# Mean and variance of four chunks through a quadratic form, and their z normalised straight out of PSUM, in a two-layer convolution kernel

## The chip, the cores and the metric

The kernel runs on one NeuronCore of a Trainium2 chip. A NeuronCore has a matrix engine (TensorE, PE in the profile), three engines for elementwise work (VectorE = DVE, ScalarE = ACT, GpSimd = POOL), SyncE (SP), which here only issues DMAs, and 16 DMA engines that all issuing engines share. Every engine works through its own instructions in order and waits on semaphores for the others. The metric is the device time of one execution in microseconds (us), and its median over several executions.

## The reference, cut to what matters

Two images of 1024 channels and 64 x 64 pixels pass two layers. Layer 0 is a deformable convolution block: a 1x1 convolution to 256 channels, a 3x3 convolution for the offsets, a bilinear gather at nine displaced places per pixel, a 1x1 convolution back to 1024 channels, with residual and ReLU. Layer 1 is what the change touches most:

```python
t = einsum('oc,bchw->bohw', Wt, x)   # 512 channels; p and g likewise
y = _rbf_kernel(t, p, g)             # a polynomial of second degree in t, with three sums per image as coefficients
z = einsum('oc,bchw->bohw', Wz, y)   # 512 -> 1024 channels
mu = mean(z, axis=(1, 2, 3)); var = mean((z - mu) ** 2, axis=(1, 2, 3))
zn = (z - mu) * rsqrt(var + EPS) * gn_w + gn_b
return zn + x
```

Mean and variance go over a whole image, so no z of an image can be normalised before all of its z is known, or at least its sum and its sum of squares.

## The kernel before, in words

Products are taken in a rounded format (fp32r). For precision every operand is split into a high part (ScalarE copies it to fp32r) and a low part (VectorE subtracts the high part), and a product is three matmuls: high x high, high weight x low, low weight x high (`product`, L194 to L196). The 8192 pixels of both images are 16 chunks of 512 (8 per image); a chunk of z has 8 tiles of 128 channels x 512 pixels, so there are 128 tiles, numbered through, and image 1 starts at tile 64. One tile is 4 x 3 = 12 matmuls of 512 columns.

The order of the work is written out by hand, as loops in one function for each engine:

- **Front (0 to about 665 us).** For each chunk: first convolution, nine products with w2 whose results (V) ScalarE copies out of PSUM and SyncE stores to memory (`store_v`), and the offsets (`offsets`, `select`, `y_shift`, `offs`). After each four chunks VectorE computes a table of gather places and weights, in three parts: `table_places`, `table_weights`, `table_entries`. GpSimd gathers with indirect DMAs (L631, L635), and VectorE and ScalarE weight and add what was gathered (`f_gather`).
- **Middle (about 665 to 1895 us).** For each chunk c the twelve groups of products g, p, t (`project`, q = 0 to 11), the rest of the gathers (`p_gather`), and layer 0's last convolution for the next chunk: `transposes` at q = 0 and 3, `o2` on ScalarE, `o2_low` on VectorE, `expand_pair` from q = 5. In chunk 0 the weights of the twelve groups are still being loaded in pieces `stage(w)`, w = 2 to 13, into three buffers in turn, by ScalarE's queue; ScalarE and VectorE split each piece (`split_high`, `split_low`). Pieces 5 and 6 are split ahead of q = 0.
- **End (about 1895 us on).** For each chunk GpSimd loads t into one buffer (TB). y is formed in four slices k: ScalarE scales (`y_scale`, L892), VectorE multiplies (`y_square`, L1319), ScalarE takes the high part (`y_high`, L904), VectorE the low one (`y_low`, L1323). TensorE forms z; ScalarE copies each tile to SBUF (`z_evict`, L967), VectorE takes its statistics (`stats`, L1367). z stays in SBUF, in a ring of 71 tiles. While z of image 1 is formed, image 0 is finished: a tile of x1 is loaded, VectorE forms z*a + x1 (`add_x1`, L1402), ScalarE adds the bias (`fin`, L975), SyncE stores (L548). How many tiles have been added by each z tile is written down in `adds_by`. After the last z tile come the statistics of image 1 (`fin_mean`, `fin_scale`), and then all 64 tiles of image 1 are added and stored.

```python
            for i in range(IMGS * ZT):            # ScalarE
                if zc + 1 < ALLC and k == KIN - 2:
                    for kk in range(KCP):
                        y_high(zc + 1, kk)
                z_evict(i)
```

## Time and profile before

| what | value |
|---|---|
| median of 3 runs | 2354.85 us (2352.66 to 2355.01) |
| the profiled execution's own time | 2349.92 us |
| its span, first to last instruction | 2348.1 us |
| TensorE busy | 2237.8 us, 95% of the span |
| VectorE, ScalarE, GpSimd busy | 67%, 53%, 33% |
| mean granted TensorE clock | 0.981 |
| DMA over the span | 284 GB/s |

The profile is that of one execution. Its span leaves out 1.8 us around it. TensorE's busy time counts overlapping matmuls once; in a stream each matmul is in the trace for 0.39 us, but the next one starts 0.23 us later, and it is this spacing that sums up to the time. A granted clock of 1.00 is 2.4 GHz, 0.50 is 1.2 GHz.

### The profile page before, as it was taken

Reading aid. Unit: us, or ns where it says so; the run is one execution under the profiler, and the core shown is the slowest. Engines: PE = TensorE matmul, PEld = TensorE weight load, DVE = VectorE, ACT = ScalarE, POOL = GpSimd, SP = SyncE. Lnnn points to the kernel's source line nnn. Section 1 sums busy time; section 2 is a strip of 40 time slices with the busy share of each in tenths; the row PEclk is TensorE's granted clock in tenths of the full one; section 3 lists DMA queues with packets and bytes.
Section 4 is the critical chain, followed back from the end, with each engine's and each line's share of the span. In section 5 each row is a group of like instructions: output and inputs, shape, how many; then the busy total and the mean of one; then the engine's idle time right before and its main releaser. Section 6 shows DMA issues by size and latency. Waiting matters only on the chain.

```text
span 2348.1 us, 29804 instructions
## 1 busy us (share of the span) xinstructions
PE 2237.8 (95%) x10252; PEld 1853.9 (79%) x10252; DVE 1573.3 (67%) x3177; ACT 1254.2 (53%) x2432; POOL 771.9 (33%) x706
## 2 busy tenths in 40 slices
PE   7999999999998999999999999999999999999970
PEld 6888888887877788888888888888888878887750
DVE  4213226667578988898889988898885324457855
ACT  6444444453455565656555655565553324446745
POOL 0100002333314555465567666766661000000000
PEclk9999999999999999999999999999999999999985
DMA  8988989999998998898889888988893111118869
GB/s 305 316 312 281 310 293 385 390 400 386 362 379 280 314 338 304 309 337 306 306 310 323 306 313 306 328 307 318 302 332 132 62 48 53 54 50 286 318 230 387
DMA packets 289823, 667.97 MB, mean 284 GB/s; under 512 B 27112, under 2 KB 101608, under 8 KB 283528
## 3 DMA queue, kind: packets, MB, share of 16 engines
q0 software_dynamic: 88048, 322.81, 39.0%
q1 hardware_dynamic: 171240, 257.87, 31.0%
q10 hardware_dynamic: 30384, 85.39, 9.8%
q8 instruction: 81, 1.33, 0.2%
q14 instruction: 70, 0.57, 0.1%
HBM read 435.47 MB, written 230.49 MB: 284 GB/s over the span
## 4 chain that ended last, share of the span: by engine, by line
PE 83%; DVE 7%; DMA 6%; SPq 1%; ACT 1%; issue 1%; POOL 0%; ACTq 0%; DVEq 0%
PE bank L194 22%; PE bank L196 22%; PE bank L195 22%; PE bank L1458 5%; PE bank L1459 5%; PE bank L1460 5%; DVE z L1402 2%; DMA xs<-x 2%; PE bank L1476 2%; DVE a L1029 1%; DMA g<-vwide,tbl 1%; DMA stage<-in_wl 1%; DMA xin<-in_x 1%; DVE zst L1367 1%; PE bank L1500 0%
## 5 line engine op out<-in xcount | busy, mean ns | idle before, releaser
L631 POOL DMA_INDIRECT g<-vwide,tbl x512 | 583.4, 1139 | 542.5 <-DVE a L1029 234.1
L194 PE MATMUL bank<-x1h,wlh 128*128 128x512 f32 x1536 | 603.1, 393 | 2.5 <-DVE x1l L1291 2.5
L196 PE MATMUL bank<-x1h,wll 128*128 128x512 f32 x1536 | 600.2, 391 | 0.0
L195 PE MATMUL bank<-x1l,wlh 128*128 128x512 f32 x1536 | 599.5, 390 | 0.0
L1029 DVE SCALAR_TENSOR_TENSOR a<-g,tbl,a 128x256 f32<-128x256 f32 x1224 | 527.6, 477 | 23.1 <-DMA g<-vwide,tbl 19.4
L658 ACT ACTIVATE g<-g,tbl 128x256 f32<-128x256 f32 x1008 | 426.9, 499 | 212.7 <-DMA g<-vwide,tbl 173.9
L194 PEld LDWEIGHTS bank<-x1h,wlh 128*128 128x128 f32 x1536 | 288.7, 188 | 62.9 <-issue 2.7
L196 PEld LDWEIGHTS bank<-x1h,wll 128*128 128x128 f32 x1536 | 288.7, 188 | 62.3
L195 PEld LDWEIGHTS bank<-x1l,wlh 128*128 128x128 f32 x1536 | 289.0, 188 | 60.8
L737 ACT ACTIVATE vb<-bank 128x512 f32<-128x512 f32 (+1 forms) x320 | 174.5, 554 | 193.4 <-PE bank L1460 168.9
L1458 PE MATMUL bank<-w2h,o1h 128*128 128x512 f32 (+1 forms) x640 | 237.3, 371 | 0.0
L1459 PE MATMUL bank<-w2l,o1h 128*128 128x512 f32 (+1 forms) x640 | 236.5, 369 | 0.0
L1460 PE MATMUL bank<-w2h,o1l 128*128 128x512 f32 (+1 forms) x640 | 236.0, 369 | 0.0
L1084 DVE TENSOR_TENSOR xl<-xin,xh 128x1024 fp32r<-128x1024 f32 x64 | 78.3, 1225 | 214.1 <-ACT xh L709 213.9
L194 PE MATMUL bank<-yh,wzh 128*128 128x512 f32 x512 | 203.3, 397 | 4.0 <-DVE yl L1323 2.8
L196 PE MATMUL bank<-yh,wzl 128*128 128x512 f32 x512 | 202.0, 395 | 0.0
L195 PE MATMUL bank<-yl,wzh 128*128 128x512 f32 x512 | 201.6, 394 | 0.0
L635 POOL DMA_INDIRECT g<-vone,tbl x128 | 152.8, 1194 | 132.0 <-DVE a L1013 101.0
L1367 DVE BATCH_NORM_STATS2 zst<-z 128x6 f32<-128x512 f32 x128 | 87.3, 689 | 103.5 <-ACT z L967 103.4
L646 POOL DMA_DIRECT2D tb<-t x16 | 8.7, 544 | 447.4 <-DVE yl L1323 436.2
L1291 DVE TENSOR_TENSOR x1l<-xf,x1h 128x512 fp32r<-128x512 f32 x128 | 83.9, 687 | 104.1 <-ACT x1h L858 104.1
L1010 DVE TENSOR_TENSOR a<-a,g 128x512 f32<-128x512 f32 x224 | 152.7, 682 | 0.0
(154 smaller groups left out, 3273.6 us busy)
## 6 DMA issues: line engine op xcount, KB each, us to landing
vwide<-vb SPq DMA_DIRECT2D x256, 256.0 KB, 4.7
vwide<-vb SPq DMA_DIRECT2D x112, 512.0 KB, 4.4
xf<-in_x SPq DMA_DIRECT2D x32, 1024.0 KB, 5.5
x<-xf ACTq DMA_DIRECT2D x32, 1024.0 KB, 7.1
out<-z SPq DMA_DIRECT2D x128, 256.0 KB, 5.3
xin<-in_x ACTq DMA_DIRECT2D x54, 512.0 KB, 5.6
t<-ts ACTq DMA_DIRECT2D x64, 256.0 KB, 4.9
tb<-t POOLq DMA_DIRECT2D x16, 1024.0 KB, 5.2
```

The lines of the kernel that those rows point to most:

```text
L194: nc.tensor.matmul(out, wh, xh, start=first, stop=False)
L195: nc.tensor.matmul(out, wh, xl, start=False, stop=False)
L196: return nc.tensor.matmul(out, wl, xh, start=False, stop=last)
L631: pool.indirect_dma_start(slot[:].rearrange("p a c -> p (a c)"), None, d["vwide"][img], bass.IndirectOffsetOnAxis(ap=at[:, i, tap(u), 0:1] ...
L635: pool.indirect_dma_start(slot[:, 2 * y:2 * y + 2, :].rearrange("p a c -> p (a c)"), None, d["vone"][img], bass.IndirectOffsetOnAxis(ap=at ...
L658: ins = nc.scalar.activation(slot[:, c, :], slot[:, c, :], ACT.Copy, scale=TBL[p % 3][:, 1, tap(u), w:w + 1])
L737: nc.scalar.activation(VB[g % NVB][:, 0:n, a, :], RING[count % 4][:, 0:n * CMID].rearrange("p (t c) -> p t c", c=CMID), ACT.Copy).then_inc ...
L1010: nc.vector.tensor_tensor(acc, acc, slot[:, 0:2 * CMID], ALU.add).then_inc(half_done, 1)
L1029: ins = nc.vector.scalar_tensor_tensor(out=acc, in0=slot[:, c, :], scalar=scale, in1=acc, op0=ALU.mult, op1=ALU.add)
L1458: nc.tensor.matmul(out, oh, W2H[:, k, lo:hi], start=k == 0, stop=False)
L1459: nc.tensor.matmul(out, oh, W2L[:, k, lo:hi], start=False, stop=False)
L1460: last = nc.tensor.matmul(out, ol, W2H[:, k, lo:hi], start=False, stop=k == KMID - 1)
```

## The change

Image 1's last four chunks (12 to 15, tiles 96 to 127) are called direct, the others held.

1. **M.** From Wz (a second layout `wn`, loaded by GpSimd) TensorE forms M = Wz^T Wz, the upper triangle in 8 pieces of four blocks, ahead of chunk 11 (tile 88 = M_AT). ScalarE and VectorE split the pieces ahead of it, and M behind it; the lower triangle is mirrored by six transposes.
2. **Quadratic form.** After tile 95, for each of chunks 12 to 15 in turn, y is formed once, and TensorE forms M y (four slices by four outputs by two matmuls). VectorE multiplies it with y and sums (`q_sum`), which gives the sum of z squared. The sum of y, which with the row sums of Wz gives the sum of z, comes out of ScalarE's `y_high` as `accum_out`. The square in y is made by GpSimd here. t is loaded into TB and a second buffer TB2, whose place is that of the tiles 44 to 47. After that the statistics of image 1 are known.
3. **Direct z.** Then y of chunks 12 to 15 is loaded and formed again, TensorE forms z, and VectorE reads it from PSUM in `add_x1`, with the normalising scale; no `z_evict`, no `stats`. Held and direct tiles alternate by twos in the order of the outputs (`tile_at`, `PLACE`). Twelve SBUF places serve the direct tiles, and six PSUM banks; a bank is free when the tile in it has been added.
4. **Image 0's tiles** are added at another pace (`added_by` in place of `adds_by`).
5. **Front.** The weight pieces 5 to 13 are loaded by SyncE, behind its last V stores, with the x of chunk 1 behind the pieces 7 and 8. They are split at q = 0 to 8, two to three groups later than before. `table_places` moves from the end of iteration s = 5, 9, 13 to s = 6, 10, 14, behind `y_shift`; `table_weights` and `table_entries` move from s = 6, 10, 14 to s = 7, 11, 15, the weights behind `y_shift`, where they stood ahead of it.

```diff
@@ SyncE
+            for w in range(5, 2 + GROUPS):
+                stage(w)
+                if w in (7, 8):
+                    load_xf(1, w - 7)
@@ (loads of x1 for image 1)
-    early = [z_at[57], z_at[59], z_at[61], A_AT, A_AT + 4 * KB, R5 + 32 * KB]
-    XT = XB + [... for i, at in enumerate(early + [at + 4 * KB * i for i in range(4) for at in (R1, G_AT)])]
+    pairs = (36, 38, 40, 42, 60, 62, 33, 44, 46, 25, 28, 30)
+    XT = XB + [m.put(f"xt{i}", [128, 2, NPX], at=z_at[i]) for i in pairs]
+    DIRECTS = 12
@@ GpSimd
-            for zc in range(ALLC):
-                pool.wait_ge(t_out, 16 * KCP * (zc + 1))
-                at_least(pool, yl_done, KCP * zc)
-                pool.dma_start(TB[:], d["t"][zc]).then_inc(t_in, 16)
+            def load_t(yc):
+                zc = Y_SEQ[yc][1]
+                if yc < ALLC:
+                    pool.wait_ge(t_out, 16 * KCP * (zc + 1))
+                if tb_user(yc) is not None:
+                    pool.wait_ge(yl_done, KCP * (tb_user(yc) + 1))
+                elif tb(yc) is TB2:
+                    for tile in range(44, 48):
+                        out_of(tile)
+                pool.dma_start(tb(yc)[:], d["t"][zc]).then_inc(t2_in if tb(yc) is TB2 else t_in, 16)
+            def q_square(yc, k):
+                pool.wait_ge(u_done, KCP * yc + k + 1)
+                nc.gpsimd.tensor_tensor(tb(yc)[:, k, :], UB[k % 2][:], tb(yc)[:, k, :], ALU.mult).then_inc(u2_done, 1)
...
+            load_t(FIRST_Q)
+            for yc in range(FIRST_Q, ALLC):
+                for k in range(KCP):
+                    q_square(yc, k)
+                if yc == FIRST_Q:
+                    load_t(yc + 1)
+                load_t(yc + 2)
+            for yc in range(ALLC + 2, len(Y_SEQ)):
+                load_t(yc)
@@ ScalarE
+                if i == M_AT:
+                    for p in range(MPIECES):
+                        piece_high(p)
+                        fins(E_M + p)
+                    product_high()
...
+            for qi in range(QUADS_Z):
+                yc = FIRST_Q + qi
+                for k in range(KCP):
+                    y_scale(yc + 1, k)
+                for k in range(KCP):
+                    y_high(yc + 1, k)
+                for k in range(KCP):
+                    fins(E_Q + KCP * qi + k)
@@ VectorE
+            for qi in range(QUADS_Z):
+                yc = FIRST_Q + qi
+                for k in range(KCP):
+                    y_square(yc + 1, k)      # only for the direct z
+                for k in range(KCP):
+                    adds(E_Q + KCP * qi + k)
+                for o in range(KCP):
+                    q_sum(qi, o)
+                for k in range(KCP):
+                    y_low(yc + 1, k)
+            fin_mean_1()
+            fin_var_1()
+            fin_scale(1)
...
+                if i % 2:
+                    for pos in range(PLACE[i] - 3, PLACE[i] + 1):
+                        add_x1(pos)
@@ TensorE
+            def z_free(i):
+                if i >= DIRECT + 6:
+                    pe.wait_ge(sum_done, PLACE[i - 6] + 1)
+                elif i >= DIRECT:
+                    pe.wait_ge(qr_done, KCP * (QUADS_Z - 1) + (i - DIRECT - 3 if i - DIRECT > 3 else 0))
+                else:
+                    at_least(pe, z_ev, i - 5)
+            def piece(p):
+                pe.wait_ge(wl_done, WPIECES + p + 1)
+                high, low = MPH[p % 2], MPL[p % 2]
+                for k in range(KCP):
+                    rows, cols = slice(128 * k, 128 * k + 128), slice(128 * k, 128 * KCP)
+                    last = product(nc, ZB[k][:, 0:128 * (KCP - k)], high[:, rows], low[:, rows], high[:, cols], low[:, cols], p == 0, p == MPIECES - 1)
+                last.then_inc(mm_done, 1)
+            def quadratic(qi):
+                yc = FIRST_Q + qi
+                if qi == 0:
+                    pe.wait_ge(z_ev, DIRECT)
+                    pe.wait_ge(wl_done, WPIECES + MPIECES + 2 * KCP - 1)
+                if qi > 1:
+                    pe.wait_ge(qr_done, KCP * (qi - 1))
+                for k in range(KCP):
+                    pe.wait_ge(yh_done, KCP * yc + k + 1)
+                    for o in range(KCP):
+                        nc.tensor.matmul(q_bank(qi, o)[:], MH[k][:, 128 * o:128 * o + 128], YH[:, k, :], start=k == 0, stop=False)
+                        last = nc.tensor.matmul(q_bank(qi, o)[:], ML[k][:, 128 * o:128 * o + 128], YH[:, k, :], start=False, stop=k == KCP - 1)
+                    last.then_inc(q_done, 1)
...
+                if KIN * zc == M_AT:
+                    pe.wait_ge(z_ev, M_AT)
+                    for p in range(MPIECES):
+                        piece(p)
+                if zc == FIRST_Q:
+                    for qi in range(QUADS_Z):
+                        quadratic(qi)
...
+                    if i == M_AT + 1:
+                        mirror()
+                    if i == DIRECT + 1:
+                        partition_sums()
@@ VectorE, front
-                if s % 4 == 2 and 6 <= s < ALLC:
-                    table_weights((s - 6) // 4)
                 f_gather(s, 3)
...
                 if 2 <= s < ALLC:
                     y_shift(s - 2)
+                if s % 4 == 2 and 6 <= s < ALLC:
+                    table_places((s - 6) // 4)
+                if s % 4 == 3 and 7 <= s < ALLC:
+                    table_weights((s - 7) // 4)
```

By `added_by`, 48 of image 0's tiles have been added when tile 94 is reached, and 50 at tile 95; the quadratic form's four rounds hold 6, 5, 5 and 0 `fin` instructions. `coefficients` forms six numbers in place of three, and `split_low` of Wz's four pieces takes two row sums (`reduce_sum`) each.

## Rows read from the trace of the kernel before

**Rows 1.** The page: busy time by engine; a costly group (busy us, mean ns).
```profile
PE 2237.8 (95%) x10252; PEld 1853.9 (79%) x10252; DVE 1573.3 (67%) x3177; ACT 1254.2 (53%) x2432; POOL 771.9 (33%) x706
...
L631 POOL DMA_INDIRECT g<-vwide,tbl x512 | 583.4, 1139 | 542.5 <-DVE a L1029 234.1
```

**Rows 2.** Windows: busy us of each engine (x count), granted clock, DMA share, GB/s.
```profile
2150.00:2200.00 50.00, 48.98 (x210) 39.02 (x209) 40.28 (x63) 39.16 (x64) 1.08 (x2) 1.00 0.91 326
2250.00:2300.00 50.00, 23.97 (x103) 19.07 (x101) 32.09 (x53) 26.56 (x42) 0.00 (x0) 0.75 0.72 252
2300.00:2348.10 48.10, 0.00 (x0) 0.00 (x0) 22.33 (x34) 22.94 (x35) 0.00 (x0) 0.50 0.98 382
```

**Rows 3.** Chain that ended last, its end: start us, us, what.
```profile
2279.40 35.15 DVE z L1402 x53
...
2326.33 1.38 ACT z L975 x2
```

**Rows 4.** Timeline of PE: first product of chunk 12, last product of chunk 15.
```profile
2181.65 0.47 PE L194 MATMUL bank<-yh,wzh 128*128 128x512 f32 x1
...
2272.40 0.40 PE L196 MATMUL bank<-yh,wzl 128*128 128x512 f32 x1
```

**Rows 5.** Groups from 1640 us on: count | busy us, mean ns | idle before.
```profile
L1402 DVE SCALAR_TENSOR_TENSOR z<-z,fa,xs 128x512 f32<-128x512 f32 x64 | 46.8, 745 | 22.5 <-DMA xs<-x 22.4
L975 ACT ACTIVATE z<-z,fb 128x512 f32<-128x512 f32 x128 | 87.2, 718 | 11.3 <-DVE z L1402 10.8
L967 ACT ACTIVATE z<-bank 128x512 f32<-128x512 f32 x128 | 75.0, 593 | 132.0 <-PE bank L196 123.8 <-DMA out<-z 6.8
L892 ACT ACTIVATE ub<-tb,coef 128x512 f32<-128x512 f32 x64 | 51.4, 807 | 3.8 <-DMA tb<-t 3.4
L904 ACT ACTIVATE yh<-tb,coef 128x512 fp32r<-128x512 f32 x64 | 45.3, 721 | 26.1 <-PE bank L196 24.9 <-DVE tb L1319 0.8
L1319 DVE TENSOR_TENSOR tb<-ub,tb 128x512 f32<-128x512 f32 x64 | 44.0, 687 | 4.9 <-ACT ub L892 4.6
L1299 DVE CUSTOM_DVE_ANT_0 gs<-bank,gs,sums 128x512 f32<-128x512 f32 x15 | 11.2, 744 | 32.9 <-PE bank L196 30.6 <-issue 2.3
L866 ACT ACTIVATION_READ_ACCUMULATOR gs<-bank 128x1 f32 x14 | 2.8, 197 | 0.0
```

**Rows 6.** Timeline of PE, products of 256 columns.
```profile
579.29 0.28 PE L1458 MATMUL bank<-w2h,o1h 128*128 128x256 f32 x1
579.41 0.28 PE L1459 MATMUL bank<-w2l,o1h 128*128 128x256 f32 x1
```

**Rows 7.** The page's DMA issues: count, KB each, median us to landing.
```profile
out<-z SPq DMA_DIRECT2D x128, 256.0 KB, 5.3
...
tb<-t POOLq DMA_DIRECT2D x16, 1024.0 KB, 5.2
```

**Rows 8.** Waits of PE from 400 to 800 us: total, times, longest.
```profile
PE bank L194 <- DVE o2l L1178: 11.0, 2, 9.3
PE bank L1484 <- DVE y L1193: 4.2, 2, 2.1
...
PE bank L194 <- DVE xl L1084: 1.8, 1, 1.8
```

**Rows 9.** Windows, behind one of those waits.
```profile
570.00:580.00 10.00, 7.91 (x36) 6.42 (x35) 9.92 (x27) 2.49 (x5) 4.16 (x4) 0.83 1.04 384
```

**Rows 10.** Timeline of DVE: the ten instructions of the table's weights.
```profile
403.45 0.43 DVE L1147 TENSOR_TENSOR tab<-gtt 128x144 f32<-128x144 f32 x1
...
406.95 0.31 DVE L1153 TENSOR_TENSOR pos<-pos 128x144 f32<-128x144 f32 x1
```

**Rows 11.** Timelines of ACT and of SP's queue, about 670 us.
```profile
678.62 1.06 ACT L687 ACTIVATE wlh<-stage 128x1024 fp32r<-128x1024 f32 x1 [8.28 <-DMA stage<-in_wl]
...
684.89 1.06 ACT L687 ACTIVATE wlh<-stage 128x1024 fp32r<-128x1024 f32 x1 [3.59 <-DMA stage<-in_wl]
...
669.16 5.49 SPq L462 DMA_DIRECT2D vone<-vb  x4
```

More of the change, by code:

```diff
@@ L310, in program, with q_bank, tb, tb_user @@
     PT, PM = BANK[0], BANK[1]
+    def q_bank(qi, o):
+        return ((ZB[0], ZB[1], ZB[2], ZB[3]), (ZB[4], ZB[5], PT, PM))[qi % 2][o]
+    def tb(yc):
+        return TB2 if yc in (FIRST_Q + 1, FIRST_Q + 3) else TB
+    def tb_user(yc):
+        return max((i for i in range(yc) if tb(i) is tb(yc)), default=None)
+    def t_ready(eng, yc):
+        eng.wait_ge(t2_in if tb(yc) is TB2 else t_in, 16 * sum(1 for i in range(yc + 1) if tb(i) is tb(yc)))
+    def z_slot(i):
+        return i % ZRING if i < DIRECT else 48 + (i - DIRECT) % DIRECTS
+    def mirrored(b):
+        return (PT[:, 0:128], PT[:, 128:384], PM[:, 0:384])[b - 1]
+    def raw_piece(p):
+        run = next(r for r, (lo, hi) in enumerate(RAW_RUNS) if lo <= p < hi)
+        return RAW[run][:, p - RAW_RUNS[run][0], :]
     def o2_tiles(n):
@@ L516, in _ @@
                         load_xf(0, h)
+                if s > 4 and s % 4 == 0:
+                    table((s - 8) // 4)
                 if s:
@@ new lines, in fins, with out_of, piece_high @@
+            def fins(e):
+                for j in range(added(e - 2), added(e - 1)):
+                    fin(j)
+            def out_of(tile):
+                act.wait_ge(out_done[tile % NOUT], 16 * (tile // NOUT + 1))
+            def piece_high(p):
+                run = next(r for r, (lo, hi) in enumerate(RAW_RUNS) if lo <= p < hi)
+                act.wait_ge(raw_in[run], 16)
+                if p < 2:
+                    out_of((25, 27)[p])
+                else:
+                    act.wait_ge(mm_done, GROUPS * ALLC + p - 1)
+                nc.scalar.activation(MPH[p % 2][:], raw_piece(p), ACT.Copy).then_inc(wh_done, 1)
@@ new lines, in mirror_high @@
+            def mirror_high():
+                act.wait_ge(tr_done, TILES * ALLC + KCP - 1)
+                for b in range(1, KCP):
+                    nc.scalar.activation(MH[b][:, 0:128 * b], mirrored(b), ACT.Copy).then_inc(wh_done, 1)
+            for i in range(DIRECT):
+                zc, k = divmod(i, KIN)
+                if i == M_AT:
[3 more added lines that the diff above has]
+                    product_high()
+                if k == KIN - 2:
+                    for kk in range(KCP):
+                        y_high(zc + 1, kk)
+                z_evict(i)
+                if i == M_AT + 2:
+                    mirror_high()
+                if 2 <= k < 2 + KCP:
+                    y_scale(zc + 1, k - 2)
+                if i == ZT + 3:
+                    fin_std()
+                if i >= ZT:
+                    fins(event(i))
@@ L978, in _ @@
+            for qi in range(QUADS_Z):
[6 more added lines that the diff above has]
+                    fins(E_Q + KCP * qi + k)
+            for j in range(added(len(ADDED) - 2), ZT):
+                fin(j)
+            fin_std_1()
+            for i in range(DIRECT, IMGS * ZT):
                 zc, k = divmod(i, KIN)
@@ L980, in _ @@
                     for kk in range(KCP):
-                        y_high(zc + 1, kk)
-                z_evict(i)
+                        y_high(y_index(zc + 1), kk)
                 if zc + 1 < ALLC and 2 <= k < 2 + KCP:
-                    y_scale(zc + 1, k - 2)
-                if i == ZT + 3:
-                    fin_std(0)
-                for j in range(adds_by(i - ZT - 2), adds_by(i - ZT - 1)):
-                    fin(j)
-            fin_std(1)
-            for i in range(ZT, IMGS * ZT):
-                fin(i)
+                    y_scale(y_index(zc + 1), k - 2)
+                if i % 2 and i > DIRECT + 1:
+                    for pos in range(PLACE[i] - 7, PLACE[i] - 3):
+                        fin(pos)
+            for pos in range(IMGS * ZT - 4, IMGS * ZT):
+                fin(pos)
         @block.vector
@@ L1328, in _ @@
                 x1_low(0, k)
[L1329 to L1330 removed]
+            split_low(4)
             for c in range(ALLC):
```

370 lines of the change are left out of this document (267 added, 103 removed).

## Prediction, on record before the changed kernel was run

> **What bounds the kernel now.** I read the page first: TensorE is busy for 95% of the span [rows 1], so only what it waits for, what it is given to do, and what lies outside its work can move the end. The windows of the last 200 us come next: TensorE is full until 2250, stops inside the next window, and from 2300 on does nothing, while the DMA share is 0.98 at 382 GB/s [rows 2]. The timeline gives the stop: the last product starts at 2272.40 and takes 0.40, so it ends at 2272.8 [rows 4]. The span ends at 2348.1: a tail of **75.3 us** in which the 64 tiles of image 1 are added and stored. The chain of waits shows it as VectorE's 53 adds in a row (35.15 us) and the last `fin` at 2326.3, with 20 us of queued stores behind it [rows 3]. Ahead of the tail the last 32 tiles take 2272.8 - 2181.65 = **91.2 us** of TensorE [rows 4]. Then the waits of TensorE in the front: 11.0 us for `o2_low` (9.3 in one), 4.2 for `y_shift`, 1.8 for `x_low` [rows 8].
>
> **The end, part by part.** t counts from the end of tile 95, 2181.6 before.
>
> *M.* TensorE may start when the banks are clear. Behind chunk 10's last product ScalarE has in its queue one `y_high` (0.72), two `z_evict` (0.59 each), three `fin` (0.72 each) and `piece_high` (a copy of the same shape, 0.59) [rows 5]; then VectorE subtracts (0.69, by `y_square` [rows 5]). 0.72 + 1.18 + 2.16 + 0.59 + 0.69 = 5.3 us. A piece is three products each of 512, 384, 256 and 128 columns. 512 columns are 0.23 us (91.2 us / 384 products = 0.237 with the waits [rows 4]), 256 are 0.12 [rows 6], 384 I put between at 0.175, and 128 at no more than 0.12: 3 x 0.645 = 1.93, times 8 = 15.4 us. ScalarE (0.59 + 0.72) and VectorE (0.69 + 0.75) stay under 1.93 per piece. Splitting M is hidden behind tiles 88 and 89. A wait of this length leaves the clock low: behind a wait of 2.1 us the granted clock was 0.83 over 10 us [rows 9], that is 3.4 us at half rate, 1.7 lost. M costs 5.3 + 15.4 + 1.7 = **22.4** (15.4 if the pieces are ready; 28 if the loads of image 0's x hold VectorE, which waited 22.4 us for them before [rows 5]).
>
> *Quadratic form.* Its products are 4 x 32 x 0.23 = 29.6 us, but I expect ScalarE's order of work, not TensorE, to set the pace. After t = 0: `y_high` 0.9 with the read of the accumulator (0.2 [rows 5]), `z_evict`, two `fin`, `z_evict`: 3.4 us, then chunk 12's form, to about 10.8. Chunk 13's t goes to TB2, where tiles 44 to 47 lie. Tile 47's `fin` comes last in that queue, at 4; its store lands 5.3 later, and only then does GpSimd issue the load, which takes 5.2 [rows 7]: with some 0.7 for issuing, y of chunk 13 starts at **15.5**. Four `y_scale` (0.81) wait in turn for GpSimd's squares, which the trace does not show. Bounds: 0.69, as VectorE takes [rows 5], and 2.3, twice GpSimd's 1.14 for an indirect DMA [rows 1]; I take 1.1, near that row. Two buffers then give 4.1 us for the four, and the first `y_high` is done 0.9 later: 5.0 from start to TensorE's start. The four `y_high` end at 7.6, then come 6, 5, 5 `fin` at 0.65 back to back. So TensorE starts chunk 13 at 20.5, 14 at 15.5 + 7.6 + 3.9 + 5.0 = 32.0, 15 at 27.0 + 7.6 + 3.3 + 5.0 = 42.9, and ends at 50.3. VectorE has meanwhile squared chunk 12's second y, then takes `q_sum` 4 x 0.74 and one `y_low` [rows 5]: direct z starts at **55.5**. Of this TensorE idles 26 us. If squares take 0.69 it is 52, at 2.3 it is 63; if the load of t were not late, 44.
>
> The Trainium skill (GPSIMD Engine Reference, section 3.1) has GpSimd 1.96 times slower than VectorE in a two-input operation; twice 0.687 would be an estimate of 1.35 us a square, and the sum would be about 1.5 us longer. No row here shows it.
>
> *Direct z.* The statistics' product stands behind tiles 96 and 97 in TensorE's queue; the chain of small VectorE instructions before it fits into those 5.6 us, 0.8 added. The rest of it overlaps tiles 98 to 101, for which banks are free. 32 tiles again take 91.2; the clock is low at first (2.0, as above). VectorE's 64 adds (0.75) and eight `y` slices per chunk are about 65 us, ScalarE's less: both hidden. After the last tile: two adds 1.5, `fin` 0.7, a store 5.3 [rows 5, 7] = **7.4** where 75.3 stood. The stores now run beside TensorE: from t = 53 the queues carry 16.8 MB out, 15.7 MB of x1 and 3 MB of t; at 382 GB/s [rows 2] that is 93 us, to 146, and TensorE ends at 55.5 + 94 = 149.5. This is nearly a tie, so I add 1 us.
>
> Sum: 22.4 + 55.5 + 0.8 + 2.0 + 7.4 + 1.0 = 89.1 in place of 75.3: the end costs **+14**. Bounds: M 15 to 28, form 44 to 63, DMA 0 to 10 more: -5 to +37, though the ends do not come together.
>
> **The front.** Removed: the ten instructions of `table_weights` ahead of `y_shift`, 403.45 to 407.26 = 3.8 us [rows 10], more than each of the two waits of 2.1 that TensorE had there [rows 8]; `table_places` no longer stands ahead of `x_low` (1.8); and the clock lost 1.7 behind the second wait [rows 9]. Together 7.7. Given back: weights and entries (about 3.8 each) now stand in s = 11, both ahead of the `x_low` that chunk 12's first products need; no row tells how much of these 7.6 us slack there hides; I take 2 (0 to 7.6). And all of this runs at a DMA share above 1 [rows 9], so I count **4.5**, not 5.7.
>
> Weights by SyncE: ScalarE waited 8.3 and 3.6 us for pieces 5 and 7 [rows 11], and VectorE and the gathers behind it, which is why `o2_low` came 9.3 late. Now one gather unit runs first. But SyncE is held by its V stores until 669.16 + 5.49 = 674.65 [rows 11], and the piece lands some 3 us later than it did. Net of that, the unit (3.3), and one split less before `o2_low` (1.2): 1.5, plus the quicker refill behind it: **3.5**, with 0 and 11 (all of it, and the clock) as bounds. Behind that TensorE runs without a wait to the end, where the seven moved pieces (needed three groups later) have 16 us of cover; without it each would cost its landing, 7.
>
> The Trainium skill (Trainium Kernel Development and Optimization, Key Constraints) says that DMAs from SP, ACT and POOL queues run on the same 16 engines and that another issuer saves only the issuing. By it this part would give about nothing. The trace differs in what it shows: what is lost is ScalarE's wait, not its issuing.
>
> Small: row sums of Wz (eight, about 0.7) and three more coefficients lie on VectorE in chunk 15, beside full TensorE; two splits late would show there. Image 0's faster adds (5/3 a tile for 3/2) lie beside z.
>
> Front -8, end +14: **+6**. Against the profiled span 2348.1 that is 2354; its own time lies 4.9 below the median of the runs shown (2349.92 to 2354.85), so the forecast is 2354.85 + 6 = **2361 us**.
>
> **Rivals.**
> 1. *Slower by 5 to 12* (0.40): the above.
> 2. *Faster* (0.20): the front gives all it holds. The gathers restart as soon as ScalarE no longer waits, the 9.3 vanishes with its 1.7 of clock, and nothing of the tables comes back: 7.7 + 11 + 1.7 (the smaller `o2_low` wait [rows 8]) = 20, and 14 - 20 = -6: 2349. It decides once the front gives more than 19. For it: ScalarE's two waits are 11.9 us [rows 11]. Against it: DMAs were saturated.
> 3. *No change* (0.25): front 8 as counted, but the form's rounds are shorter (squares at 0.69, `fin` hidden) and the clock holds: end +8, 2355.
> 4. *Much slower* (0.15): the overlap of stores and z does not work as meant. Stores, x1 and t share the engines at the 326 GB/s of the mixed stage [rows 2], 109 us from t = 53, or GpSimd needs 2.3 a square: +10 more, 2371.
>
> A measurement of this kernel can tell about 0.2% (4.7 us) from no change. Faster by more: 0.20. Within: 0.25. Slower: 0.55. Range 2346 to 2373: it takes in rival 2's half and most of 4's; that of the likeliest alone is 2357 to 2367.
>
> **What would show it.** In the profile after: no wait of TensorE for `y_shift` in the front, and a new one of 1 to 3 us at `x_low` of s = 11 or 12; the wait for `o2_low` near 700 us smaller than 9.3, and how much; some 5 us idle ahead of M; M's pieces 15 us; TensorE idle about 9, 4 and 4 us between the forms, the first behind t into TB2, the others behind ScalarE; GpSimd's square near 1.1 us; a last store 7 to 8 us behind the last product. Wrong I would be if the form ran at TensorE's pace, if the front gave over 15, or if the stores fell behind z.

## The result, and the profile after

| | us |
|---|---|
| before, median of 5 runs | 2354.85 (2352.59 to 2357.48) |
| after, median of 5 runs | 2379.21 (2376.41 to 2379.35) |
| after / before | **1.0102**, 95% interval 1.0088 to 1.0116 |
| forecast | 2361, range 2346 to 2373 |
| profiled span, before and after | 2348.1 and 2377.2 |
| profiled execution's own time, before and after | 2349.92 and 2379.26 |

The change makes the kernel 24 us slower. The sign was the forecast one, the size four times what I had forecast, and the time lies outside my range. The two profiles differ by 29 us, the medians by 24: the profiled execution of before was 4.9 us under its median, that of after stood on it.

TensorE is busy for longer than before [rows 1], and GpSimd now has arithmetic to do. This is the page's list of busy times, and the group of the new squares in the stretch from 2180 to 2270 us (count, busy us, mean ns, idle before):

```profile
PE 2293.9 (96%) x10480; PEld 1900.2 (80%) x10480; DVE 1598.8 (67%) x3231; ACT 1264.7 (53%) x2466; POOL 824.7 (35%) x729
```

```profile
L763 POOL TENSOR_TENSOR tb<-ub,tb 128x512 f32<-128x512 f32 x16 | 21.1, 1340 | 48.5 <-ACT ub L1028 48.5
```

The windows of the last 230 us of after, where [rows 2] had three (busy us and count of PE, PEld, DVE, ACT and POOL, then granted clock, DMA share, GB/s). In order: the wait before M, M, chunk 11, the four rounds of the form, and the direct z:

```profile
2150.00:2166.00 16.00, 0.50 (x3) 0.06 (x1) 8.89 (x15) 7.20 (x12) 2.12 (x4) 0.63 0.94 347
2166.00:2184.00 18.00, 17.51 (x96) 16.26 (x97) 10.49 (x16) 8.71 (x14) 0.00 (x0) 0.85 0.84 277
2184.00:2207.00 23.00, 23.00 (x104) 18.54 (x103) 16.66 (x25) 16.49 (x34) 5.32 (x4) 1.00 0.60 195
2207.00:2227.00 20.00, 7.81 (x34) 5.93 (x32) 6.85 (x10) 6.83 (x12) 4.61 (x5) 0.89 0.53 186
2227.00:2247.00 20.00, 9.90 (x32) 7.64 (x32) 11.51 (x18) 9.77 (x19) 6.14 (x6) 0.76 0.61 210
2247.00:2265.00 18.00, 10.10 (x32) 7.82 (x32) 11.14 (x15) 9.47 (x20) 6.53 (x7) 0.69 0.59 204
2265.00:2280.00 15.00, 10.43 (x33) 8.20 (x34) 14.62 (x30) 10.55 (x19) 0.80 (x1) 0.73 0.76 253
2280.00:2371.00 91.00, 91.00 (x385) 73.10 (x384) 63.15 (x106) 56.41 (x87) 1.65 (x3) 0.98 0.96 371
```

The last window is the change doing what it should: TensorE is full for 91 us while stores and loads go on beside it at 371 GB/s. The four rounds of the form are the opposite: in the first three no engine is busy for more than two thirds of the time, and in all four the DMA engines are idle for a quarter to nearly half of it. (In the fourth VectorE is busy for 14.62 of 15 us; it is taken up below.) Such a stretch is bound by waiting, and the timeline of PE says for whom (start, duration, what, in brackets the idle time before it and what ended it). The rows are: M's first product, the first product of each of the four chunks' forms, the first direct z, the last product.

```profile
2166.49 0.77 PE L247 MATMUL bank<-mph 128*128 128x512 f32 x1 [15.99 <-DVE mpl L1592]
2210.43 0.50 PE L1960 MATMUL bank<-yh,mh 128*128 128x512 f32 x1 [3.15 <-ACT z L1103]
2227.69 0.80 PE L1960 MATMUL bank<-yh,mh 128*128 128x512 f32 x1 [9.72 <-ACT yh L1049]
2247.66 0.76 PE L1960 MATMUL bank<-yh,mh 128*128 128x512 f32 x1 [10.08 <-ACT yh L1049]
2265.13 0.77 PE L1960 MATMUL bank<-yh,mh 128*128 128x512 f32 x1 [7.37 <-ACT yh L1049]
2279.47 0.76 PE L247 MATMUL bank<-yh,wzh 128*128 128x512 f32 x1 [4.45 <-DVE yl L1542]
2371.12 0.40 PE L249 MATMUL bank<-yh,wzl 128*128 128x512 f32 x1
```

The new tail, in place of the 75.3 us behind [rows 4], from the timeline of all engines:

```profile
2370.94 1.46 DVE L1689 SCALAR_TENSOR_TENSOR z<-bank,fa,xt 128x512 f32<-128x512 f32 x2 [2.83 <-PE bank L249]
2371.73 1.43 ACT L1117 ACTIVATE z<-z,fb 128x512 f32<-128x512 f32 x2 [2.85 <-DVE z L1689]
2372.47 1.04 SPq L650 DMA_DIRECT2D out<-z  x2
```

The last product ends at 2371.52 and the span at 2377.2: 5.7 us.

The front: waits of PE from 400 to 800 us (answers [rows 8]), the first and the sixth group of the offsets' products from 400 us on (before: at 411.94 and 614.60) and the first z product, and ScalarE's wait for a weight piece (answers [rows 11]):

```profile
PE bank L247 <- DVE o2l L1388: 9.1, 2, 8.0
PE bank L247 <- DVE x1l L1501: 3.5, 1, 3.5
```

```profile
410.07 0.96 PE L1803 MATMUL bank<-sel,y 108*128 108x18 f32 x8
...
606.64 0.96 PE L1803 MATMUL bank<-sel,y 108*128 108x18 f32 x8
...
1901.42 0.47 PE L247 MATMUL bank<-yh,wzh 128*128 128x512 f32 x1 [1.20 <-DVE sums L1512]
```

```profile
674.51 1.06 ACT L821 ACTIVATE wlh<-stage 128x1024 fp32r<-128x1024 f32 x1 [11.63 <-DMA stage<-in_wl]
```

The waits for `y_shift` and for `x_low` are gone, and the product at 614.60 is at 606.64; SyncE's weight loads come only behind this, so the tables gave these 8.0 us. z starts at 1901.42 where it started at 1910.68: the whole front gave 9.3 in this pair of profiles.

**Where the 23 us between forecast and profile went.** The stretch from the end of tile 87 (2150.51) to the first direct z (2279.47) is 129.0 us. By my terms it was 5.3 (idle) + 43.3 (M's work and clock 17.1, chunk 11 22.8, the first form's wait 3.4) + 52.1 (form) = 100.7. It is 15.99 + 43.9 + 69.0. So 10.7 us are missing in M's idle, 16.9 in the form, 0.6 between them. Round by round the form was forecast as 17.1, 11.5, 10.9 and 12.6 us and took 17.3, 20.0, 17.5 and 14.3, so nearly all of the 16.9 lies in the second and third. The direct z took 92.05 for my 95.0, the tail 5.7 for 7.4, and tile 87 ended 7.6 us sooner than before for my 8. 28.2 - 3.0 - 1.7 + 0.4 = 23.9, against 2377.2 - 2354.1 = 23.1.

**Why M waited.** The chain that ended last, in order of time (start us, us, what), ahead of M:

```profile
2155.39 0.73 ACT z L1117
2156.14 9.41 DMA out<-z
2165.65 0.70 DVE mpl L1592
2166.49 0.77 PE bank L247
```

The split pieces lie in z places 25 to 28. Image 0's tiles there had only just had their `fin`, and a store issued at 2156 landed 9.4 us later, with the DMA engines at 0.94.

**Why the form's rounds were long.** The same chain through the first two rounds:

```profile
2210.24 0.66 DVE z L1689
2211.18 5.63 DMA out<-z
2216.88 0.47 issue
2217.37 5.22 DMA tb<-t
2222.62 0.82 ACT ub L1028
2223.51 2.50 POOL tb L763 x2
...
2226.84 0.45 ACT yh L1049
...
2229.75 1.84 ACT z L1117 x3
2231.74 3.90 DMA xs<-x
...
2239.68 2.09 DVE sq L1542 x3
...
2242.30 0.58 POOL tb L759
2242.89 3.00 POOL tb L763 x2
```

and the waits of that stretch, 2207 to 2280 us (us in total, times, longest):

```profile
DVE z L1689 <- DMA xs<-x: 27.9, 6, 16.3
PE bank L1960 <- ACT yh L1049: 27.2, 3, 10.1
POOL tb L759 <- DVE sq L1542: 25.3, 2, 13.8
```

First round: store, load of t, scaling, squares, `y_high`: the late TB2 that I had forecast. From there on it is a ring through the queues of four engines, each turn of it one round later. VectorE's adds of a round stand ahead of its sums and wait 16.3 us for a load of x; SyncE has that load behind `store_out`; the store waits for a `fin`, which ScalarE does behind the four `y_high`; these wait for GpSimd's squares; GpSimd has `load_t` of the next chunk ahead of them, and that waits for the `y_low` behind VectorE's adds.

The fourth round is another matter: no y follows in it. Its 32 products ran at a low clock for 9.9 us, to 2275.02, and VectorE, busy with hardly a break since 2266, started the sums of that chunk at 2275.89; both were late together. VectorE had lost time to something that no term of mine held (its and GpSimd's timeline):

```profile
2260.52 5.83 DVE L1689 SCALAR_TENSOR_TENSOR z<-z,fa,xs 128x512 f32<-128x512 f32 x1
2260.86 4.94 POOL L763 TENSOR_TENSOR tb<-ub,tb 128x512 f32<-128x512 f32 x4
```

An add of 0.75 us took 5.83: it started 0.3 us before GpSimd's four squares and ended 0.5 us behind them. e3, with its adds in the same place, shows the same (5.82 us); in e2 and e5, with the adds moved, the longest add is 1.8 us. That the squares held it is my reading; no run made the squares elsewhere. Here it cost the end under 1 us, since the sums had to wait for the products until 2275.02 in any case.

### The profile page after: what moved, and what is told of

Its sections match the earlier page's. It is cut to its first block, busy times and chain, and to the rows that moved or that the text cites. A ratio compares the mean times of both kernels' runs of the same rounds, so it can differ in the third digit from the quotient of the medians.

```text
span 2377.2 us, 30451 instructions
## 1 busy us (share of the span) xinstructions
PE 2293.9 (96%) x10480; PEld 1900.2 (80%) x10480; DVE 1598.8 (67%) x3231; ACT 1264.7 (53%) x2466; POOL 824.7 (35%) x729
## 3 DMA queue, kind: packets, MB, share of 16 engines
q8 instruction: 82, 1.34, 0.2%
## 4 chain that ended last, share of the span: by engine, by line
PE 88%; DMA 4%; DVE 3%; SPq 2%; issue 1%; ACT 1%; POOL 0%; DVEq 0%; ACTq 0%; POOLq 0%
PE bank L247 23%; PE bank L248 23%; PE bank L249 23%; PE bank L1777 5%; PE bank L1778 5%; PE bank L1779 5%; PE bank L1795 2%; DMA xs<-x 1%; DMA out<-z 1%; DMA g<-vwide,tbl 1%; DMA vwide<-vb 1%; SPq L545 1%; SPq L546 0%; PE bank L1819 0%; DVE z L1689 0%
## 5 line engine op out<-in xcount | busy, mean ns | idle before, releaser
L734 POOL DMA_INDIRECT g<-vwide,tbl x512 | 607.6, 1187 | 515.5 <-DVE a L1234 215.4
L759 POOL DMA_DIRECT2D tb<-t x20 | 10.9, 545 | 458.7 <-DVE yl L1542 409.0
L1215 DVE TENSOR_TENSOR a<-a,g 128x512 f32<-128x512 f32 x224 | 153.6, 686 | 0.6 <-ACT g L792 0.6
L1218 DVE TENSOR_TENSOR a<-a,g 128x512 f32<-128x512 f32 x224 | 153.7, 686 | 0.0
```

Source lines behind the costliest of these rows:

```text
L734: pool.indirect_dma_start(slot[:].rearrange("p a c -> p (a c)"), None, d["vwide"][img], bass.IndirectOffsetOnAxis(ap=at[:, i, tap(u), 0:1] ...
L1218: nc.vector.tensor_tensor(acc, acc, slot[:, 2 * CMID:4 * CMID], ALU.add).then_inc(g_used[1], 1)
```

## The experiments

Ratios are to the kernel before, timed beside each run on the same chip; the change's own is 1.0102. The chips differ (before's median was 2353.6 us beside e1 to e4, 2380.2 beside e5 to e8, 2353.1 beside e9 to e12 and 2362.8 beside e13 to e15, and in the second and fourth group its runs spread over 24 and 20 us), so the stretch from tile 87's end to the first direct z, read from each timeline of PE, is the firmer measure. It is given in three parts: idle before M, M's first product to the form's first, form to direct z.

| run | idle | M to form | form | stretch | ratio (95%) |
|---|---|---|---|---|---|
| the change | 16.0 | 43.9 | 69.0 | 129.0 | 1.0102 (1.0088 to 1.0116) |
| e1_own_pieces | 10.5 | 45.8 | 68.3 | 124.5 | 1.0086 (1.0069 to 1.0103) |
| e2_adds_last | 16.5 | 44.3 | 61.3 | 122.0 | 1.0071 (1.0054 to 1.0088) |
| e3_early_tb2 | 15.9 | 46.4 | 59.8 | 122.1 | 1.0064 (1.0047 to 1.0080) |
| e5_all_three | 10.1 | 45.9 | 51.3 | 107.3 | 1.0042 (1.0018 to 1.0067) |
| e6_reordered | 10.7 | 45.7 | 56.1 | 112.5 | 1.0055 (1.0033 to 1.0077) |
| e7_pool_order | 10.9 | 45.0 | 51.4 | 107.2 | 1.0016 (0.9994 to 1.0037) |
| e9_adds_earlier | 10.1 | 48.2 | 48.6 | 106.9 | 1.0011 (0.9997 to 1.0024) |
| e10_adds_earlier_reordered | 8.3 | 50.5 | 56.0 | 114.8 | 1.0043 (1.0028 to 1.0057) |
| e13_raw_order | 8.4 | 45.5 | 51.4 | 105.4 | 1.0008 (0.9990 to 1.0027) |
| e14_adds_before_form | 9.6 | 52.6 | 48.0 | 110.2 | 1.0041 (1.0019 to 1.0062) |
| e15_both | 9.4 | 53.0 | 47.2 | 109.5 | 1.0029 (1.0007 to 1.0051) |
| e11_no_front | 16.0 | 44.3 | 67.0 | 127.4 | 1.0165 (1.0143 to 1.0186) |

**e1: M's pieces off the z places.**

```diff
-    MPH, MPL = ([m.put(f"{n}{i}", [128, KCP * 128], f32r, at=z_at[at + 2 * i]) for i in range(2)] for n, at in (("mph", 25), ("mpl", 26)))
+    MPH = [m.put(f"mph{i}", [128, KCP * 128], f32r, at=R5 + 32 * KB + 2 * KB * i) for i in range(2)]
+    RAWL = [m.put(f"rawl{r}", [128, n, KCP * 128], f32r, at=z_at[at]) for r, (n, at) in enumerate(((4, 20), (3, 17), (1, 24)))]
...
-                if p < 2:
-                    out_of((25, 27)[p])
-                else:
+                if p >= 2:
                     act.wait_ge(mm_done, GROUPS * ALLC + p - 1)
...
-                out_of(33)
-                out_of(34)
+                for tile in (25, 26, 27, 28, 33, 34):
+                    out_of(tile)
```

> M's pieces no longer lie in z places 25 to 28: the two high parts lie in the two idle u buffers, the low parts take the place of their raw pieces; the waits for the stores of tiles 25 to 28 move to the copy of the finished product. Nothing else changes. Theory (M's idle is the wait for stores that had only just been issued): TensorE stands 6 to 9 us before M instead of 16.0, since the raw loads, issued 4 us after the last product of tile 87, are then the next thing late; the end comes 6 to 9 us sooner than with the change (2370 to 2373). Rival (the stores of image 0 set the pace whatever lies where, and the wait comes back at the copies into places 25 to 34): M starts sooner but the first form starts at most 2 us sooner, the total stays at 2377 to 2381.

M's idle fell from 16.0 to 10.5, and two later waits for pieces (0.57 and 1.74 us) gave 2 back: 4.4 us of the stretch, 1.0086 for 1.0102. The idle lies above the theory's 6 to 9 us and the time (2373.6) just above its 2373: those stores did hold M, but 10 us of the wait were held by something else as well.

**e2: VectorE's adds last in each round.**

```diff
-                for k in range(KCP):
-                    adds(E_Q + KCP * qi + k)
                 for o in range(KCP):
                     q_sum(qi, o)
                 for k in range(KCP):
                     y_low(yc + 1, k)
+                for k in range(KCP):
+                    adds(E_Q + KCP * qi + k)
```

> In each round of the form VectorE does the four or five adds of image 0 after the sums with the banks and the low parts of the next y, not ahead of them; same work. Theory (a ring: adds wait for x loads, these stand behind stores in SyncE's queue, the stores behind the last pass, which ScalarE does behind the high parts of y, and the next round's sums and low parts stand behind the adds): the third and fourth round fall from 17.5 us each toward 11 to 13, and the time by 8 to 13 us (2366 to 2371). Rival (the rounds are as long as ScalarE's scaling, GpSimd's four squares of 1.24 us and the four high parts of 0.9 us behind each other, about 11 us, and the load of t): the time falls by at most 3 us (2376 to 2379). The first round, whose idle 9.72 us is the late load of y 13's t, stays as it is by both.

The form's chunks start at 2209.3, 2226.3, 2239.3 and 2254.5: the second and third rounds are 13.0 and 15.2 us where they were 20.0 and 17.5, the form 7.8 shorter, the ratio 1.0071 (7 us below the change). The ring's theory holds, at the lower end of what it gave (2370.8 us for 2366 to 2371). The fourth round became longer, 16.0 us for 14.3. VectorE still waits for x, but nothing of the form stands behind it (waits of 2209 to 2271 us):

```profile
DVE z L1689 <- DMA xs<-x: 12.5, 3, 6.4
ACT z L1117 <- DVE z L1689: 10.1, 4, 4.8
```

The second row is what took the wait's place: ScalarE stands at a `fin`, with the scaling of the next t behind it.

**e3: the second t buffer on places 36 to 39.**

```diff
-    TB2 = m.put("tb2", [128, KCP, NPX], at=z_at[44])
+    TB2 = m.put("tb2", [128, KCP, NPX], at=z_at[36])
-    pairs = (36, 38, 40, 42, 60, 62, 33, 44, 46, 25, 28, 30)
+    pairs = (44, 46, 40, 42, 60, 62, 33, 36, 38, 25, 28, 30)
...
-                    for tile in range(44, 48):
+                    for tile in range(36, 40):
                         out_of(tile)
```

> The second t buffer lies on z places 36 to 39 instead of 44 to 47 and waits for those stores; the two x1 buffers that lay there change places with it. Theory (the 12.8 us for which GpSimd's queue waits with the load of y 13's t are the stores of tiles 44 to 47): TensorE's idle 9.7 us before the second chunk's form falls to 0 to 2 us, and the time by 7 to 10 us (2369 to 2372). Rival (the ring of adds and loads takes it back in the next rounds, whose sums stand behind adds that are no earlier): the second form starts 8 us sooner, the third at most 3 us sooner, and the time falls by 0 to 3 us (2376 to 2379).

GpSimd loads t of chunk 13 at once, and that of chunk 14 5 us later (timeline of POOL):

```profile
2205.80 0.58 POOL L759 DMA_DIRECT2D tb<-t  x1
2210.83 0.55 POOL L759 DMA_DIRECT2D tb<-t  x1 [4.45 <-DVE sq L1542]
```

The second form starts 9.0 us after the first (before this edit 17.3), the later rounds stay near what they were (18.8, 17.6, 14.4 for 20.0, 17.5, 14.3), the form is 9.2 shorter, the ratio 1.0064 (2369.5 us). The theory is confirmed and the rival refuted, though the stretch ahead of the form was 2.5 us longer in this profile (46.4 for 43.9), so that the whole is 6.9 shorter.

**e5: all three.**

> The three edits together: M's pieces off the z places, VectorE's adds last in each round, the second t buffer on z places 36 to 39. One by one they cut the profiled stretch from the end of tile 87 to the first direct z (129.0 us with the change) by 3.7, 7.8 and 9.3 us. Theory (three separate waits, each of which stood on the path of the form by itself): the gains add up, the stretch is 107 to 110 us and the time 2356 to 2360. Rival (they are pieces of one wait for image 0's stores and loads, so that one takes what another gives): the stretch is 115 to 120 us, the time 2364 to 2370.

The stretch is 107.3 us, 21.7 below the change: the three add up (4.4 + 7.0 + 6.9 = 18.3 by the stretches one by one, and 3.4 more; the 7.8 and 9.3 in the expectation are e2's and e3's gains in the form alone, not in the stretch, and e1's is 4.4, not 3.7). The timed runs alone do not decide between the two expectations. The ratio is 1.0042 (1.0018 to 1.0067), on a chip on which before itself took 2380 us; of the 2353.6 for which they were written, the theory's 2356 to 2360 would be 1.0010 to 1.0027, the rival's 2364 to 2370 1.0044 to 1.0070.

**e6 and e7: two more orders.** e7 puts GpSimd's squares ahead of `load_t` of the chunk after; e6 does this and has ScalarE scale, then do the last passes of the round before, then the high parts.

```diff
                 for k in range(KCP):
                     q_square(yc, k)
-                if yc == FIRST_Q:
-                    load_t(yc + 1)
-                load_t(yc + 2)
+                load_t(yc + 1)
```

> The three edits, and two orders changed: GpSimd squares chunk n's four tiles before it loads t of chunk n+1 and never waits with a load ahead of squares that are due; ScalarE scales the next t before it does the last pass of the round before, and that ahead of the high parts. Theory (with the adds out of the way, the rest of a round is the order of scaling, squares and last passes): the rounds fall to 9 to 11 us each, the half-clock forms to under 8.5, and the time to 2350 to 2355. Rival (SyncE loads x only four tiles ahead of its stores, and the stores wait for the later last passes, so VectorE's adds and the sums behind them wait longer): no better than the three edits alone, 2357 to 2364.

> The three edits, and GpSimd's order alone: the four squares of chunk n+1 ahead of the load of t of chunk n+2. Theory (the load holds up the squares, 3 to 6 us of GpSimd waiting for the low parts in each round): 2 to 6 us faster than the three edits alone. Rival (the squares wait for ScalarE's scaling, which is behind the last passes, and a later load makes the next scaling late): same within 2 us, or up to 4 us slower.

e7's stretch is that of e5 within 0.1 us: once the adds are last, GpSimd's order costs nothing in it. (Its timed median is 4 us under e5's, 2385.9 for 2389.8, but the intervals of the two ratios overlap.) e6 differs from e7 in ScalarE's order alone and is 5.2 us longer: the rival. The reason that it gave, later last passes, hence later stores and later loads of x, is plainest in e10 below.

**e9, e10, e14: image 0's adds moved out of the form** (into chunk 11; 20, 20 and 24 there for 12).

```diff
     for i in range(KIN):
-        cum.append(cum[-1] + 1 + i % 2)
+        cum.append(cum[-1] + 2 + i % 2)
```

That is e9's; e10 is the same edit on top of e6, and e14 has `+ 3`.

> The three edits, and 8 more of image 0's tiles are added in chunk 11 (20 instead of 12), so that the form's rounds have 6 left instead of 14; same work. Chunk 11's 23 us moved data at 60% of the DMA engines in the change's profile, so there is room. Theory (what is left of the rounds, 51 us for four where TensorE's own work is 29, is image 0's adds, last passes and loads between the form's steps): first form to first direct z falls to 40 to 44 us, the stretch from tile 87's end from 107 to 96 to 101, the time against the three edits by 6 to 11 us. Rival (the rounds are scaling, squares and high parts on their own): the form stays at 49 to 52 us, the time within 2 us of the three edits. Second rival (the adds put off chunk 11's z): what the form gains chunk 11 loses.

> As the run before it, with ScalarE's last passes a round later and GpSimd's squares ahead of its loads. With the three edits alone these two orders made the form 5 us longer, since x loads waited for the later last passes. Theory (with 6 adds left in the form that ring is gone): the form is 36 to 41 us, 2 to 5 us under the run before it. Rival (the load of t then sets the rounds, being behind the squares): 42 to 47 us, slower than the run before it.

> The three edits, and 24 of image 0's adds in chunk 11 (3 a tile), so that only 2 of the 64 are left for the form's rounds. With 20 in chunk 11 the rounds took 9.5, 17.4, 9.8 and 11.9 us, and the 17.4 was the one in which adds, x loads and last passes still stood between the steps. Theory (a round without image 0's work takes 9.5 to 10): the form is 38 to 42 us instead of 51.3, chunk 11 gives back 3 to 6 of it (24 adds are 18 us of VectorE beside its other 11 in 23 us), the stretch is 99 to 103 us. Rival (the long round is chunk 14's own, late t and squares, whatever image 0 does): the form stays at 46 to 51 us and the stretch is 107 or more.

By the form's length my theory of e9 missed by 5 us, that of e14 by 6, that of e10 by 15, and e10's rival (42 to 47) by 9. In e10 the third form waited 15.9 us for `y_high`; by the chain of its trace three last passes at 2231.4 are followed by a load of x of 8.2 us, an add at 2241.7, a last pass, and only then by the high parts at 2243.1. In e9 the rounds are 9.5, 17.4, 9.8 and 11.9 us, in e14 10.8, 14.9, 10.3 and 12.1. The long round is not image 0's volume alone, since e14 has only two adds left in it. Its form (48.0) and stretch (110.2) are what its rival gave, under which the long round is chunk 14's own. The trace points at where the two adds stand. e14's timeline of all engines:

```profile
2236.40 2.73 DVE L1545 SCALAR_TENSOR_TENSOR sq<-tb,coef,yh 128x512 f32<-128x512 f32 x4
2239.05 1.40 DVE L1689 SCALAR_TENSOR_TENSOR z<-z,fa,xs 128x512 f32<-128x512 f32 x2
...
2239.82 1.38 ACT L1122 ACTIVATE z<-z,fb 128x512 f32<-128x512 f32 x2 [4.48 <-DVE z L1689]
...
2241.11 1.50 ACT L1033 ACTIVATE ub<-tb,coef 128x512 f32<-128x512 f32 x2
...
2242.00 4.94 POOL L768 TENSOR_TENSOR tb<-ub,tb 128x512 f32<-128x512 f32 x4 [1.77 <-ACT ub L1033]
...
2246.26 0.76 PE L1960 MATMUL bank<-yh,mh 128*128 128x512 f32 x1 [7.28 <-ACT yh L1054]
```

Two adds stand behind the low parts, two `fin` wait 4.5 us for them, and the scaling of chunk 14's t stands behind the `fin`, with TensorE's 7.3 us idle at the end of it. No run moved these two, so this stays a reading of the trace. And what the form gained, chunk 11 gave back (e9's second rival): M to form went from 45.9 to 48.2 and 52.6, the first form waiting 6.6 and 10.2 us for ScalarE's `z_evict`.

**e13 and e15: the order of M's raw loads.**

```diff
-    RAW_RUNS = ((0, 4), (4, 7), (7, 8))
+    RAW_RUNS = ((0, 3), (3, 7), (7, 8))
...
-                for tile in ((20, 21, 22, 23), (17, 18, 19), (24,))[r]:
+                for tile in ((17, 18, 19), (20, 21, 22, 23), (24,))[r]:
                     out_of(tile)
```

The buffers' places are exchanged with them; e15 is this edit with e14's.

> The three edits (pieces off the z places, adds last, second t buffer on places 36 to 39), and the raw pieces of Wz in another order: the first load takes the three z places 17 to 19, whose stores land first, the second the four places 20 to 23; before it was the other way round. Theory (what is left of M's wait, 10 us, is the first raw load standing behind the store of tile 23): M starts 4 to 6 us behind tile 87 instead of 10.1, and the stretch from tile 87's end to the first direct z falls from 107.3 to 101 to 104 us. Rival (ScalarE's and VectorE's queued work of chunk 10 ends no sooner, or the loads crawl at the full DMA share): 9 to 10 us, nothing gained.

> Both of these edits on top of the three. Theory (two separate waits): the stretch is 93 to 99 us, where the change has 129.0, and the time 6 to 12 us under before's: 2341 to 2349 for a before of 2354. Rival (image 0's stores are what both wait for, so starting M sooner only makes chunk 11 wait more): the stretch is 101 to 105, the time within 0.2% of before's.

The first raw load is issued 4.4 us before tile 87 ends, and M still stands 8.4 us: 1.7 gained, and the stretch (105.4) misses the theory's 101 to 104: mostly the rival. ScalarE copies the first piece at 2168.66, 5.1 us after tile 87's end, behind its evictions and `fin`; VectorE splits it at 2171.09, behind adds and the last tile's statistics. e15 gains nothing clear on e14 (109.5 us for 110.2) and lies above both of its expectations; that image 0's work is what both wait for fits this, but is not shown by it.

**e4, e8, e11, e12: the front alone, its parts, and the change without it.** e4 and e8 and e12 are the kernel before with the front's edits (both, tables, weights); e11 is the change with the front as before. The tables' edit in VectorE's slabs, as e8 has it:

```diff
-                if s % 4 == 2 and 6 <= s < ALLC:
-                    table_weights((s - 6) // 4)
...
                     y_shift(s - 2)
+                if s % 4 == 2 and 6 <= s < ALLC:
+                    table_places((s - 6) // 4)
+                if s % 4 == 3 and 7 <= s < ALLC:
+                    table_weights((s - 7) // 4)
```

> The kernel before, with the front part of the change alone: the table steps moved by a slab, the weight loads issued by SyncE, and the splits' new places. No quadratic form, no direct z. Theory (the front's gain of 9.3 us, read as the first z product after x1's sums at 1901.4 instead of 1910.7, is the front's alone and is kept to the end): 2343 to 2347, ratio 0.995 to 0.997. Rival (z is bound by the loads and stores of its stage, and what it starts sooner it ends no sooner): 2350 to 2355.

> The kernel before with the table steps moved by a slab, nothing else. Theory (tables are most of the front's gain: in the profile of the change the last slabs start 8.0 us sooner, the weight loads add 1.3 us): 2343 to 2347 where the whole front gave 2340.7. Rival (the two edits overlap, each alone gives nearly the whole gain, since the first project stage waits for weights anyway): 2340 to 2342; second rival (the weight loads are most of the gain): 2348 to 2353.

> The change without its front part: tables, weight loads and splits as in the kernel before, with the quadratic form, the direct z and the new order of the outputs. Theory (front and form are independent, the front is worth 8 to 13 us): 8 to 13 us above the change, 2386 to 2392 where before has 2354. Rival (z before M is bound by image 0's stores, which eat what the front gives, so without the front M starts hardly later): 2380 to 2384.

> The kernel before with the weight loads issued by SyncE and their splits moved, tables as they were. Theory (the front's two parts add up, and the tables give most): 1 to 4 us faster than before, ratio 0.998 to 1.000. Rival (SyncE's queue, behind the stores of V, brings the first weights later, so alone it costs): 0 to 4 us slower.

e4: 2340.71 us against 2353.62, ratio **0.9942** (0.9926 to 0.9959): 13 us faster, the fastest version here, faster than both kernels and than my theory (2343 to 2347). e11 says the same from the other side: 1.0165 - 1.0102 of 2353 is 15 us by the ratios, 2389.94 - 2353.13 = 36.8 against the change's 24.4 is 12.4 by the medians. The front is worth 12 to 15 us by timed runs, 7.6 by the pair of profiled spans (2348.1 and 2340.5), of which before's lay 4.9 under its median. Weights alone give 0.9989 (0.9979 to 0.9999), 2.6 us; tables alone 0.9932 (0.9906 to 0.9957), on the chip that spread most: more than either expectation gave, and, within its interval, all of the front's gain or most of it.

## Why the prediction was wrong, step by step

The two steps that failed are M's idle and the form's later rounds. M's idle and work together were 33.6 us, and the form, from the end of tile 95 to direct z, 72.2; my bounds were 15 to 28 and 44 to 63. By the timed medians the end cost 37 us for my 14, and the front gave 13 for my 8, so the front's surplus hid some of the miss.

- **M idle, 5.3 us: failed** (16.0). I counted what stood in ScalarE's and VectorE's queues, not the waits inside those instructions. `piece_high` and `piece_low` wait for the stores of tiles 25 to 28. I had applied just this rule to TB2 (a `fin`, then a store's landing) and not to M. e1 took 5.5 of it away. Of the rest e13 shows that the raw loads hold 1.7; that the last 3 us over my 5.3 are image 0's adds and last passes in the two queues is read from e13's timeline, and was not tried.
- **M's work, 15.4 + 1.7: right.** 2166.49 to 2184.2 is 17.7, at a granted clock of 0.85.
- **The first round (TB2): right in kind.** From the end of tile 95 at 2207.28, chunk 13 was forecast to start at 20.5 and started at 20.4. e3 shows the cause.
- **The later rounds, 11.5 and 10.9 us: failed** (20.0 and 17.5). I let chunk 14's t start as soon as ScalarE was free. VectorE's adds, which I had down as hidden, stood ahead of its sums and low parts, and closed a ring with SyncE's loads, ScalarE's last passes and GpSimd's loads. e2 takes 7 to 8 us of it away. A round with two of image 0's last passes in it took 9.8 (e9's third), one with nothing of image 0 10.3 (e14's third), so 11 was about the length without the ring. My sum also does not come out of its terms: they give 15.2 for the start of chunk 13's y, where I wrote 15.5, and 54.0 for 55.5 at its end. These 1.5 to 1.8 us have no source, and made the forecast better, not worse.
- **GpSimd's square, 1.1 us: low.** 1.34 on average and one every 1.24 when four follow each other. By the ratio in the Trainium skill (GPSIMD Engine Reference, section 3.1) my estimate had been 1.35: the trace agrees with the page and not with my nearest row. It cost under 1 us a round.
- **The half clock inside the form: left out.** I charged the clock for M and for the direct z only. With waits of 7 to 10 us between the chunks TensorE was granted 0.69 to 0.76 of 2.4 GHz, and a chunk's 32 products took 9.9 to 10.1 us for the 7.5 of the first chunk's. In the second and third round it hides, since the next chunk's y was what came last; in the fourth, where none follows, it stands in the 14.3 us, beside VectorE, which came as late.
- **Direct z and the tail: right.** 92.05 for 95.0 and 5.7 for 7.4; the nearly tied stores (0.96 of the DMA engines) did not come last.
- **The front, 8: right in the profile (9.3; 8.0 at the offsets), low in the timed runs (13).** The split was off: tables were 8.0 of it and not 4.5, since nothing came back in s = 11 or 12, where I had forecast a new wait; weights, as what is left of the pair's 9.3, 1.3 and not 3.5. In e12, with the weights alone, the waits for `o2_low` sum up to 11.3 us, as before (11.0), so no trace shows where its 2.6 us come from. ScalarE waited 11.6 us for its piece instead of 8.3, so the load did come 3 us later, as I had said. The Trainium skill (Trainium Kernel Development and Optimization, Key Constraints) would have put this part at nothing; e12's 2.6 us, with an interval from 0.2 to 5, lies little above that.

Rival 4 (2371, chance 0.15) was nearest, but not for its reasons: the stores did not fall behind z and the square was not 2.3 us.

In none of the versions tried does the change pay, its waits mended or not. The old tail's 75.3 became 5.7, 69.6 us saved. The quadratic form costs the stretch of 105.4 to 107.3 us less chunk 11's 22.8, 83 us or more. The front's 13 us make that a draw with before (1.0008 to 1.0042), and they lose to the front alone.

## What to carry to other kernels

When a new step lies in memory that is being drained, write beside each of its instructions which landing it waits for; an engine's queue counted only by durations is a lower bound. When a round passes work between all engines, look for a queue in which work that nothing waits for (adds of another image) stands ahead of work that the round waits for, and follow it round until it closes. A change in two parts should be timed in two: here one part gave 13 us and the other took 37.

## What I had not expected of the hardware

- A 256 KB store that takes 5.3 us in the median [rows 7] took 9.4 at a DMA share of 0.94 (347 GB/s), and this was what M waited for.
- An add on VectorE took 5.83 us in place of 0.75 where it ran beside four squares on GpSimd (4.94 us).
- The same kernel before took 2353 us on two chips, 2363 and 2380 on two others, and the two slower ones also spread more from run to run. In the profiles from the chip of 2380 us (e5 to e8) TensorE has lost time in the stage of gathers, 700 to 1900 us: it is busy there for 1177 to 1185 us, where before has 1189, and the change and e4 1195 to 1196.
